# One step of eight transformer batches: the router part of the shared feed-forward computed in two groups of tokens, and GpSimd's scaling of the normalised rows placed behind a rotary sum

## The chip, the cores and the metric

The program runs on one NeuronCore of one Trainium2 chip. The metric is the device time of one execution in microseconds (us). Five engines work beside each other: TensorE (PE in the profile, with its weight loads as PEld), VectorE (DVE), ScalarE (ACT), GpSimd (POOL) and SyncE (SP, which here only starts transfers). They meet through semaphores.

## The reference

An adaptive-normalisation transformer block over 8 batches of 512 tokens by 256 features, all in float32: low-rank attention, then a mixture of 16 experts with a shared feed-forward.

```
h = layernorm(x) * (1 + ca) + sa
x = x + ga * attention(h)              # 16 heads, rotary part of 64, low-rank keys, causal
h = layernorm(x) * (1 + cb) + sb
scores = softmax(h @ gate_w.T)         # 16 experts, the best 4 of each token
y = sum over the 4 experts of weight * (silu(h @ w_gate) * (h @ w_up)) @ w_down
shared = silu(h @ sw_gate) * (h @ sw_up) @ sw_down     # 352 inner features
x = x + gb * (y + shared)
```

sa, ca, ga, sb, cb, gb are six modulation vectors of each batch. An expert takes at most 128 tokens, the first of all 4096 in order that choose it.

## The kernel before, in words

Nothing schedules this program: each engine's instructions are written out in the order in which they run, in one function per engine, and every dependence is a semaphore wait in that text. The 512 tokens of a batch are 4 tiles of 128. The 16 heads are 8 pairs. PSUM is one tensor `PS` of 8 banks of 128 x 512 float32.

For each batch the engines go through eight `step`s, one per head pair (project the next pair's queries, scores, maxima, exponentials, transposes, values), and then a `middle`, which ends the attention of batch b and prepares batch n = b + 1. There are seven such middles in the loop, and an eighth, the last, which has no next batch (`pre` is False). The middle is the place of the change. On TensorE it does, in this order:

- the next batch's low-rank projections (L815), the last pair's values (L695), the output projection by token tile (`output`, L785), and transposes of keys and latents (L834);
- `q_project(0, ..., (0, 1))` (L626 to L630), the first pair's queries of the next batch, first half, into bank 6;
- `turn_h2` (L761): transposes of the second normalised rows `h2`, tiles 0 to 2, into banks 1 and 2. It waits for `n2_ready`, which DVE raises behind `normed` (L1173);
- `q_project(0, ..., (2, 3))`, second half, into bank 7;
- `turn_h2_last` (L766): transposes of tile 3 into bank 0, behind the second `n2_ready`;
- `ffn(b, 2, (3, 4))` (L776, L778): the third part of the shared feed-forward, 96 inner features, whose weights carry the 16 router columns beside them. All 512 tokens are the moving columns, two halves of the 256 features are summed, and each waits for its half of `h2T`;
- `q_turn` (L639): eight transposes of the first pair's queries, which wait for `nope_ready` and `rope_ready`;
- `ffn` parts 0 and 1, with the transposes of the router's logits (L800) between them, and then the first scores of the next batch.

A float32 matmul over features is two instructions in the trace (the two `ffn` lines each issue one pair per half of the features).

ScalarE copies between: `turned_h2` (L1024) writes `h2T` for tiles 0 to 2 with the modulation folded in, `turned_h2_last` (L1030) for tile 3, then `nope_copy` (L951) copies the unrotated half of the queries out of banks 6 and 7 and raises `nope_ready`, and then come `tanh_gate` (L1010) and the router's logits (L1062).

VectorE normalises tile 3 (L1173) and then runs `q_rope`: it waits for `nope_ready`, makes three products out of PSUM (L1196 to L1198) and adds the two halves in SBUF (L1210), which raises `rope_ready`. After that come `silu_mid` (L1282, L1284), `q_low` (L1248) and the router's scores.

GpSimd raises the normalised rows to a power for the standard deviation (L464), and once `h2` has been transposed it multiplies `h2` by the modulation row (L483) and adds the other (L485), 1024 elements a partition each, for SyncE to store as the rows that the experts gather later. Then it copies `x_in` to `x_res` (L489). After the last middle the experts run: GpSimd scatters the tokens' entries, gathers rows, and TensorE computes expert by expert.

`x1_ready` counts the three pieces of the residual of a batch that DVE has formed out of PSUM; the third piece reads bank 3.

Of the kernel before, what the change touches and what calls it, by code (L numbers as in the profile page):

```python
# [23 lines left out]
P = 128  # L24
# [53 lines left out]
def adaln_block(nc, x, wkva, wqnT, wqpe, wkT, wvT, wo, qgam, kgam, sgate, sup, sdown,  # L78
# [21 lines left out]
    with ExitStack() as ctx:  # L100
# [330 lines left out]
        def _(pool):  # L431
# [42 lines left out]
            def post(b, n):  # L474

                wait_alone(pool, var2_ready, NT * b + 3)
                root(rstd2[:, 0:3], mv2[:, 0:3, 1], LN_EPS, eps2, rs2_ready, 2 * b)
                wait_alone(pool, var2_ready, NT * (b + 1))
                root(rstd2[:, 3:], mv2[:, 3:, 1], LN_EPS, eps2, rs2_ready, 2 * b + 1)
                spread = lambda i: modb[:, i, :].unsqueeze(1).to_broadcast([P, NT, H])  # L480
                pool.wait_ge(n2_ready, 2 * (b + 1))
                pool.wait_ge(h2T_ps, 3 * (b + 1))
                pool.tensor_tensor(h2[:], h2[:], spread(2), ALU.mult).then_inc(h2_scaled, 1)  # L483
                pool.wait_ge(h2_scaled, b + 1)
                pool.tensor_tensor(h2[:], h2[:], spread(1), ALU.add).then_inc(h2_ready, 1)  # L485
                if n is not None:
                    wait_alone(pool, x1_ready, 3 * (b + 1))
                    wait_alone(pool, x_landed, (b + 2) * 16)
                    pool.tensor_copy(x_res[:], x_in[:]).then_inc(res_ready, 1)  # L489
# [90 lines left out]
        def _(pe):  # L580
# [188 lines left out]
            def ffn(b, m, banks):  # L769

                off, w = MT[m]
                wide = w + (NE if m == 2 else 0)
                for c in range(2):
                    if m == 2:
                        pe.wait_ge(h2T_ready, 4 * b + c + 3)
                    pe.matmul(PS[0:wide, banks[0], :], sg_sb[:, c, off:off + wide], h2T[:, c, :],  # L776
                              start=c == 0, stop=c == 1)
                    mm = pe.matmul(PS[0:w, banks[1], :], su_sb[:, c, off:off + w], h2T[:, c, :],  # L778
                                   start=c == 0, stop=c == 1)
                mm.then_inc(gu_ps, 1)  # L780

            def output(t, bank, pairs):

# [19 lines left out]
            def middle(b, n, post, pre):  # L803

                if pre:
                    pe.wait_ge(hT_ready, 2 * (n + 1))
                    if not post:
                        pe.wait_ge(wk_in, 4 * 16)
                        pe.wait_ge(wql_ready, 1)
                    for k, t in enumerate(KV_ORDER):  # L810
                        if post:
                            pe.wait_ge(*((pT_act, 4 * n * NPAIR - 1), (pT_dve, 2 * n * NPAIR - 1),
                                         (pT_act, 4 * n * NPAIR), (pT_dve, 2 * n * NPAIR))[k])
                        for c in range(2):
                            mm = pe.matmul(PS[:, t, 0:FW], hT[:, c, bass.ts(t, P)], wkva_sb[:, c, :],  # L815
                                           start=c == 0, stop=c == 1)
                        mm.then_inc(kv_ps, 1)
                if post:
                    values(b * NPAIR + NPAIR - 1, b)
                    pe.wait_ge(oT_ready, (b + 1) * NPAIR)  # L820
                    output(1, 7, (NPAIR - 2,))
                    output(0, 6, range(0, NPAIR - 1))
                    pe.wait_ge(oT_ready, (b + 1) * NPAIR + 1)
                    output(1, 7, (NPAIR - 1,))
                    output(0, 6, (NPAIR - 1,)).then_inc(attn_ps, 1)
                    output(2, 5, range(0, 2))
                else:
                    absorb_output()
                    pe.wait_ge(wvo_ready, 4)
                if pre:  # L830
                    pe.wait_ge(k_ready, n + 1)
                    for bank, src in ((2, kmat[:]), (1, qn[:, :, 0:P]), (0, qn[:, :, P:2 * P])):
                        for t in range(NT):
                            mm = pe.transpose(PS[:, bank, bass.ts(t, P)], src[:, t, :], ident[:])  # L834
                        mm.then_inc(kq_ps, 1)
                if not post:
                    pe.wait_ge(wql_ready, 4)
                if post:
                    output(2, 5, range(2, NPAIR)).then_inc(attn_ps, 1)
                    output(3, 3, range(NPAIR)).then_inc(attn_ps, 1)  # L840
                if pre:
                    pe.wait_ge(kql_ready, 3 * (n + 1))
                    q_project(0, n * NPAIR, (0, 1))
                if post:
                    pe.wait_ge(n2_ready, 2 * b + 1)
                    turn_h2()
                if pre:
                    q_project(0, n * NPAIR, (2, 3))
                if post:
                    pe.wait_ge(n2_ready, 2 * b + 2)  # L850
                    turn_h2_last()
                    ffn(b, 2, (3, 4))
                if pre:
                    q_turn(n * NPAIR)
                if post:
                    if pre:
                        ffn(b, 0, (5, 0))
                    turn_router(b)
                    if not pre:
                        ffn(b, 0, (5, 0))  # L860
                    pe.wait_ge(mid_ready, 3 * b + 1)
                    ffn(b, 1, (3, 4))
                    pe.wait_ge(mid_ready, 3 * b + 2)
                    pe.wait_ge(ls_ready, b + 1)
                if not pre:
                    ranks(b)
                if pre:
                    scores(n * NPAIR, True, (0, 1, 2))
                else:
                    pe.wait_ge(mid_ready, 3 * b + 3)  # L870
                    shared_down(0)
                    pe.wait_ge(slot_ready, b + 2)
                    shared_down(1)
# [64 lines left out]
        def _(act):  # L938
# [88 lines left out]
            def turned_h2_last(b):  # L1027
                act.wait_ge(h2T_ps, 3 * b + 3)
                for c in range(2):
                    act.activation(h2T[:, c, S - P:S], PS[:, 0, bass.ts(c, P)], ACT.Identity,  # L1030
                                   scale=mod2[:, 2 + c:3 + c], bias=mod2[:, c:c + 1]).then_inc(h2T_ready, 1)

            def middle(b, n, post, pre):
# [19 lines left out]
                    act.activation(ql1t[QR:P, :], PS[QR:P, 0, :], ACT.Copy).then_inc(kqh_ready, 1)  # L1053
                if post:
                    turned_h2(b)
                    turned_h2_last(b)
                if pre:
                    nope_copy(n * NPAIR)
                if post:
                    tanh_gate(b, 0, 2, 3)  # L1060
                    w = MT[2][1]
                    act.activation(lgT[:], PS[w:w + NE, 3, :], ACT.Copy).then_inc(lg_ready, 1)  # L1062
# [471 lines left out]
```

## Time and profile before

| | us |
|---|---|
| median of 3 runs | 1312.83 |
| lowest and highest run | 1309.52, 1313.0 |
| the profiled execution | 1317.52 |
| its span, first to last instruction | 1315.6 |

The profiled execution is 1.92 us longer than its span, and 4.69 us (0.36%) above the median of the other runs. In the span PE is busy for 91%, DVE 64%, ACT 51% and POOL 24%; the mean granted TensorE clock is 0.956 of full speed. In the page's 40 slices PE is nine tenths busy or more from the third to the 35th (66 to 1151 us), and the experts' part at the end is sparse on every engine. Idle time in brackets in a row stands just before its first instruction, with what ended it.

### The profile page before, as it was taken

How to read it: one execution, taken by the hardware profiler on the slowest of the kernel's cores; microseconds unless marked ns; L12 is line 12 of the kernel's file. 1: busy time of each engine (PE TensorE's matmuls, PEld its weight loads, DVE VectorE, ACT ScalarE, POOL GpSimd, SP SyncE). 2: the span in 40 equal slices, each digit the busy share in tenths (PEclk: the TensorE clock that was granted, in tenths of full speed). 3: DMA queues.
4: the chain of work that ended last, by engine and by line, in shares of the span. 5: the costliest groups of instructions: out<-in, count | busy, mean ns of one | idle time of the engine just before them, and what ended most of it. 6: DMA issues, size and time to landing. Idle time of an engine off the chain costs nothing.

```text
span 1315.6 us, 25838 instructions
## 1 busy us (share of the span) xinstructions
PE 1193.0 (91%) x7492; PEld 954.0 (73%) x7492; DVE 840.3 (64%) x2575; ACT 667.9 (51%) x1922; POOL 311.8 (24%) x366
## 2 busy tenths in 40 slices
PE   6699999999999999999999999999999999982672
PEld 4488867887688768886888778876887688741341
DVE  3367757776777668766877577767776687641221
ACT  1367635764466536762576356744666367610210
POOL 1000031221312122113221222213221222125674
PEclk7789999999999999999999999999999999986886
DMA  9100002000010001000100020000100010005563
GB/s 306 40 1 0 0 6 60 0 0 0 16 48 0 0 16 48 0 0 16 48 0 0 0 64 0 0 0 16 48 0 0 16 32 1 0 20 144 146 132 47
DMA packets 44853, 41.86 MB, mean 32 GB/s; under 512 B 10800, under 2 KB 41496, under 8 KB 44832
## 3 DMA queue, kind: packets, MB, share of 16 engines
q1 hardware_dynamic: 24864, 26.58, 6.7%
q0 software_dynamic: 7936, 6.38, 2.9%
q10 hardware_dynamic: 12032, 8.65, 2.3%
q8 instruction: 10, 0.16, 0.1%
q14 instruction: 11, 0.09, 0.0%
HBM read 30.84 MB, written 10.81 MB: 32 GB/s over the span
## 4 chain that ended last, share of the span: by engine, by line
PE 76%; DVE 8%; issue 5%; POOL 4%; DMA 3%; ACT 2%; POOLq 0%; DVEq 0%; SPq 0%; ACTq 0%
PE PS L674 10%; PE PS L695 10%; PE PS L653 7%; PE PS L654 6%; PE PS L655 6%; PE PS L785 6%; PE PS L639 4%; PE PS L815 3%; PE PS L793 3%; PE PS L776 2%; PE PS L626 2%; DMA out<-x_res,toku 2%; PE PS L629 2%; PE PS L627 2%; PE PS L630 2%
## 5 line engine op out<-in xcount | busy, mean ns | idle before, releaser
L961 ACT ACTIVATE probs<-probs,nmax 128x512 f32<-128x512 f32 (+3 forms) x512 | 283.1, 554 | 126.7 <-DVE nmax L1217 123.4
L1217 DVE CUSTOM_DVE_ANT_0 probs<-PS,cmask 128x512 f32<-128x512 f32 (+3 forms) x512 | 229.4, 488 | 101.2 <-PE PS L655 98.3
L527 POOL DMA_INDIRECT tab_dram<-entry,slot x128 | 126.1, 985 | 404.5 <-PE PS L695 372.0
L653 PE MATMUL PS<-kTh,qTh 128*128 128x512 f32 (+3 forms) x512 | 178.8, 349 | 1.2 <-DVE qTl L1248 0.6
L970 ACT ACTIVATE pT<-PS 128x384 f32<-128x384 f32 (+3 forms) x320 | 127.7, 462 | 78.9 <-PE PS L674 78.8
L674 PE MATMUL PS<-ident,probs 128*128 128x128 f32 x1280 | 166.1, 276 | 0.0
L655 PE MATMUL PS<-kTh,qTl 128*128 128x512 f32 (+3 forms) x512 | 165.4, 323 | 0.0
L654 PE MATMUL PS<-kTl,qTh 128*128 128x512 f32 (+3 forms) x512 | 165.4, 323 | 0.0
L695 PE MATMUL PS<-pT,kmat 128*64 128x512 f32 (+3 forms) x1024 | 152.0, 439 | 0.3 <-issue 0.3
L674 PEld LDWEIGHTS PS<-ident,probs 128*128 128x128 f32 x1280 | 142.8, 141 | 10.3 <-issue 7.4
L695 PEld LDWEIGHTS PS<-pT,kmat 128*64 128x64 f32 x1024 | 68.0, 136 | 76.0 <-issue 62.1
L785 PE MATMUL PS<-wvo,oT 128*128 128x256 f32 x512 | 116.4, 381 | 0.0
L1248 DVE TENSOR_TENSOR qTl<-PS,qTh 128x512 fp32r<-128x512 f32 x128 | 87.3, 687 | 36.2 <-ACT qTh L956 35.3
L653 PEld LDWEIGHTS PS<-kTh,qTh 128*128 128x128 f32 x512 | 97.0, 189 | 15.2 <-issue 5.3
L785 PEld LDWEIGHTS PS<-wvo,oT 128*128 128x128 f32 x512 | 95.4, 190 | 13.7 <-issue 1.4
L1234 DVE COPY pT<-PS 128x512 f32<-128x512 f32 (+2 forms) x192 | 81.5, 462 | 33.3 <-PE PS L674 31.3
L655 PEld LDWEIGHTS PS<-kTh,qTl 128*128 128x128 f32 x512 | 97.1, 190 | 5.6
L654 PEld LDWEIGHTS PS<-kTl,qTh 128*128 128x128 f32 x512 | 97.3, 190 | 4.5 <-issue 1.7
L961 ACT ACTIVATION_READ_ACCUMULATOR probs<-probs,nmax 128x1 f32 x512 | 95.8, 187 | 0.0
L639 PE MATMUL PS<-ident,qtok 128*128 128x128 f32 x512 | 67.5, 275 | 14.0 <-DVE qtok L1210 14.0
L462 POOL TENSOR_SCALAR rstd<-mv 128x4 f32<-128x4 f32 (+2 forms) x24 | 5.5, 231 | 309.6 <-DVE mv L1169 187.3
L626 PE MATMUL PS<-wq0h,ql0h 128*128 (+1 forms) x256 | 75.7, 296 | 2.2 <-DVE ql1s L1388 2.2
(216 smaller groups left out, 2155.0 us busy)
## 6 DMA issues: line engine op xcount, KB each, us to landing
x_in<-in_x SPq DMA_DIRECT2D x8, 512.0 KB, 5.8
modb<-mod_dram SPq DMA_DIRECT2D x8, 512.0 KB, 5.4
h_dram<-h SPq DMA_DIRECT2D x8, 512.0 KB, 2.9
out<-base SPq DMA_DIRECT2D x8, 512.0 KB, 3.4
pT<-in_wo SPq DMA_DIRECT2D x1, 2048.0 KB, 11.9
tab_dram<-entry,slot POOLq DMA_INDIRECT x128
oT<-in_wqnT SPq DMA_DIRECT2D x1, 1536.0 KB, 10.1
pT<-in_egate ACTq DMA_DIRECT2D x6, 176.0 KB
```

The lines of the kernel that those rows point to most:

```text
L527: pool.indirect_dma_start(tab_dram[:, :], bass.IndirectOffsetOnAxis(ap=slot[:, j:j + 1], axis=0), entry[:, j, :], None, bounds_check=NE * ...
L626: pe.matmul(dst, ql0h[:, tok], wq0h[:, cols], start=True, stop=False)
L639: mm = pe.transpose(PS[:, QBANKS[h], bass.ts(t, P)], qtok[:, 2 * t + h, :], ident[:])
L653: pe.matmul(PS[:, bank, 0:n], qTh[:, h, rows_q], kTh[:, 0:n], start=True, stop=False)
L654: pe.matmul(PS[:, bank, 0:n], qTh[:, h, rows_q], kTl[:, 0:n], start=False, stop=False)
L655: pe.matmul(PS[:, bank, 0:n], qTl[:, h, rows_q], kTh[:, 0:n], start=False, stop=True).then_inc(s_ps, 1)
L674: mm = pe.transpose(PS[:, bank, col:col + P], probs[:, UO[u] + j * P:UO[u] + (j + 1) * P], ident[:])
L695: mm = pe.matmul(PS[h * KL:(h + 1) * KL, OBANK, j * P:S], kmat[:, j, 0:KL], pT[:, h, j, j * P:S], start=j == 0, stop=j == NT - 1)
L785: mm = pe.matmul(PS[:, bank, 0:H], oT[:, p, bass.ts(t, P)], wvo[:, p, :], start=p == 0, stop=p == NPAIR - 1)
L961: act.activation(probs[:, UO[u]:UO[u] + UW[u]], probs[:, UO[u]:UO[u] + UW[u]], ACT.Exp, scale=-1.0, bias=nmax[:, u:u + 1], accum_out=psums ...
L970: cp = act.activation(pT[:, h, 0:i + 1, bass.ts(i, P)], PS[:, bank, col:col + UW[u]].rearrange("p (j q) -> p j q", q=P), ACT.Copy)
L1217: dve.tensor_tensor_reduce(out=probs[:, UO[u]:UO[u] + UW[u]], in0=PS[:, SBANK[u], 0:UW[u]], in1=cmask[:, S - UW[u]:S], scale=-1.0, scalar= ...
```

## The change

```diff
--- before.py
+++ after.py
@@ -480,6 +480,8 @@
                 spread = lambda i: modb[:, i, :].unsqueeze(1).to_broadcast([P, NT, H])
                 pool.wait_ge(n2_ready, 2 * (b + 1))
                 pool.wait_ge(h2T_ps, 3 * (b + 1))
+                if n is not None:
+                    wait_alone(pool, rope_ready, n * NPAIR + 1)
                 pool.tensor_tensor(h2[:], h2[:], spread(2), ALU.mult).then_inc(h2_scaled, 1)
                 pool.wait_ge(h2_scaled, b + 1)
                 pool.tensor_tensor(h2[:], h2[:], spread(1), ALU.add).then_inc(h2_ready, 1)
@@ -769,15 +771,24 @@
             def ffn(b, m, banks):
 
                 off, w = MT[m]
-                wide = w + (NE if m == 2 else 0)
                 for c in range(2):
-                    if m == 2:
-                        pe.wait_ge(h2T_ready, 4 * b + c + 3)
-                    pe.matmul(PS[0:wide, banks[0], :], sg_sb[:, c, off:off + wide], h2T[:, c, :],
+                    pe.matmul(PS[0:w, banks[0], :], sg_sb[:, c, off:off + w], h2T[:, c, :],
                               start=c == 0, stop=c == 1)
                     mm = pe.matmul(PS[0:w, banks[1], :], su_sb[:, c, off:off + w], h2T[:, c, :],
                                    start=c == 0, stop=c == 1)
                 mm.then_inc(gu_ps, 1)
+
+            def ffn_router(b, part, banks):
+
+                off, w = MT[2]
+                lo, hi = (0, S - P) if part == 0 else (S - P, S)
+                for c in range(2):
+                    pe.wait_ge(h2T_ready, 4 * b + 2 * part + c + 1)
+                    pe.matmul(PS[0:w + NE, banks[0], lo:hi], sg_sb[:, c, off:off + w + NE], h2T[:, c, lo:hi],
+                              start=c == 0, stop=c == 1)
+                    mm = pe.matmul(PS[0:w, banks[1], lo:hi], su_sb[:, c, off:off + w], h2T[:, c, lo:hi],
+                                   start=c == 0, stop=c == 1)
+                return mm
 
             def output(t, bank, pairs):
 
@@ -847,9 +858,11 @@
                 if pre:
                     q_project(0, n * NPAIR, (2, 3))
                 if post:
+                    pe.wait_ge(x1_ready, 3 * b + 3)
+                    ffn_router(b, 0, (3, 4))
                     pe.wait_ge(n2_ready, 2 * b + 2)
                     turn_h2_last()
-                    ffn(b, 2, (3, 4))
+                    ffn_router(b, 1, (3, 4)).then_inc(gu_ps, 1)
                 if pre:
                     q_turn(n * NPAIR)
                 if post:
@@ -1053,10 +1066,10 @@
                     act.activation(ql1t[QR:P, :], PS[QR:P, 0, :], ACT.Copy).then_inc(kqh_ready, 1)
                 if post:
                     turned_h2(b)
-                    turned_h2_last(b)
                 if pre:
                     nope_copy(n * NPAIR)
                 if post:
+                    turned_h2_last(b)
                     tanh_gate(b, 0, 2, 3)
                     w = MT[2][1]
                     act.activation(lgT[:], PS[w:w + NE, 3, :], ACT.Copy).then_inc(lg_ready, 1)
```

`ffn` keeps parts 0 and 1. Part 2, with the router's columns, becomes `ffn_router`, which takes a group of tokens: group 0 is tokens 0 to 383, group 1 tokens 384 to 511. Group 0 is put ahead of the wait for the last normalised tile. In the loop's seven middles all parts of the change act; the last middle has no next query, so there only the split is different.

On TensorE, the stretch between the second half of the next query's projection (last row L630 before, L632 now) and the transposes of the query. Before:

```order
L630 MATMUL PS<-wq1l,ql1s 128x256
L850 REGISTER_ALU
L766 MATMUL PS<-ident,h 128x128 [waits n2_ready]
L766 MATMUL PS<-ident,h 128x128
L775 ISA
L776 MATMUL PS<-h2T,sg_sb 112x512 [waits h2T_ready]
L778 MATMUL PS<-h2T,su_sb 96x512
L775 REGISTER_ALU
L776 MATMUL PS<-h2T,sg_sb 112x512 [waits h2T_ready]
L778 MATMUL PS<-h2T,su_sb 96x512
L639 MATMUL PS<-ident,qtok 128x128 [waits rope_ready,nope_ready]
```

Now, up to the first product of group 1:

```order
L861 ISA
L786 ISA [waits x1_ready]
L787 MATMUL PS<-h2T,sg_sb 112x384 [waits h2T_ready]
L789 MATMUL PS<-h2T,su_sb 96x384
L786 REGISTER_ALU
L787 MATMUL PS<-h2T,sg_sb 112x384 [waits h2T_ready]
L789 MATMUL PS<-h2T,su_sb 96x384
L863 REGISTER_ALU
L768 MATMUL PS<-ident,h 128x128 [waits n2_ready]
L768 MATMUL PS<-ident,h 128x128
L786 REGISTER_ALU
L787 MATMUL PS<-h2T,sg_sb 112x128 [waits h2T_ready]
```

Group 0's four products of 384 columns have moved ahead of the wait for `n2_ready`, behind a new wait for `x1_ready`; behind the transposes of tile 3 four products of 128 columns are left, and the query's transposes follow them with their waits unchanged.

On ScalarE, from the first half of `h2T` (tiles 0 to 2) to the router's logits. Before:

```order
L1024 ACTIVATE h2T<-PS,mod 128x384 [waits h2T_ps]
L1023 REGISTER_ALU
L1024 ACTIVATE h2T<-PS,mod 128x384 [waits h2T_ps]
L1028 REGISTER_ALU
L1030 ACTIVATE h2T<-PS,mod 128x128 [waits h2T_ps]
L1030 ACTIVATE h2T<-PS,mod 128x128
L950 ISA
L951 ACTIVATE qtok<-PS 128x8x64 [waits q_ps]
L1010 ACTIVATE th<-PS 96x512 [waits gu_ps]
L1062 ACTIVATE lgT<-PS 16x512
```

Now:

```order
L1037 ACTIVATE h2T<-PS,mod 128x384 [waits h2T_ps]
L1036 REGISTER_ALU
L1037 ACTIVATE h2T<-PS,mod 128x384 [waits h2T_ps]
L963 ISA
L964 ACTIVATE qtok<-PS 128x8x64 [waits q_ps]
L1041 REGISTER_ALU
L1043 ACTIVATE h2T<-PS,mod 128x128 [waits h2T_ps]
L1043 ACTIVATE h2T<-PS,mod 128x128
L1023 ACTIVATE th<-PS 96x512 [waits gu_ps]
L1075 ACTIVATE lgT<-PS 16x512
```

The copy of the query's unrotated half (`qtok`) has moved ahead of the two copies of tile 3 and of their wait for `h2T_ps`.

On GpSimd, the scaling of `h2` and what follows. Before:

```order
L482 REGISTER_ALU [waits n2_ready]
L483 TENSOR_TENSOR h<-h,modb 128x1024 [waits h2T_ps]
L485 TENSOR_TENSOR h<-h,modb 128x1024 [waits h2_scaled]
L92 ISA [waits x1_ready,const_ready]
L489 COPY x_res<-x_in 128x1024 [waits x_landed,const_ready]
```

Now:

```order
L482 REGISTER_ALU [waits n2_ready]
L92 ISA [waits h2T_ps]
L485 TENSOR_TENSOR h<-h,modb 128x1024 [waits rope_ready,const_ready]
L487 TENSOR_TENSOR h<-h,modb 128x1024 [waits h2_scaled]
L92 ISA [waits x1_ready,const_ready]
L491 COPY x_res<-x_in 128x1024 [waits x_landed,const_ready]
```

The multiplication waits for `rope_ready` as well, and the addition and the copy of `x_in` stay queued behind it.

## Rows read from the trace of the kernel before

**Rows 1.** The page's table of busy time, PE, DVE, ACT, POOL.

```profile
PE 1193.0 (91%) x7492; PEld 954.0 (73%) x7492; DVE 840.3 (64%) x2575; ACT 667.9 (51%) x1922; POOL 311.8 (24%) x366
```

**Rows 2.** Chain that ended last, 155 to 235 us: start us, us, what.

```profile
191.25 0.45 ACT h2T L1030
...
193.60 2.67 DVE qtok L1210
...
197.47 0.86 PE PS L776 x2
```

**Rows 3.** Timeline of PE, 180 to 216 us: start us, us, engine line op.

```profile
189.27 0.28 PE L630 MATMUL PS<-wq1l,ql1s 128*128 128x256 f32 x1
190.41 0.44 PE L766 MATMUL PS<-ident,h 128*128 128x128 f32 x2 [0.86 <-DVE h L1173]
191.40 1.11 PE L776 MATMUL PS<-h2T,sg_sb 128*112 128x512 f32 x2 [0.55 <-ACT h2T L1030]
...
196.40 1.06 PE L639 MATMUL PS<-ident,qtok 128*128 128x128 f32 x8 [1.32 <-DVE qtok L1210]
```

**Rows 4.** Timeline of ACT, 186 to 212 us.

```profile
188.07 1.23 ACT L1024 ACTIVATE h2T<-PS,mod 128x384 f32<-128x384 f32 x2 [6.27 <-PE PS L761]
190.89 0.81 ACT L1030 ACTIVATE h2T<-PS,mod 128x128 f32<-128x128 f32 x2 [1.58 <-PE PS L766]
191.59 0.59 ACT L951 ACTIVATE qtok<-PS 128x512 f32<-128x512 f32 x1
```

**Rows 5.** Timeline of DVE, 189 to 216 us.

```profile
189.94 0.41 DVE L1173 TENSOR_SCALAR h<-x,mv,rstd 128x256 f32<-128x256 f32 x1 [1.08 <-POOL rstd L464]
192.21 0.69 DVE L1196 TENSOR_TENSOR qr<-PS,cos_sb 128x512 f32<-128x512 f32 x1 [1.86 <-ACT qtok L951]
...
193.60 2.66 DVE L1210 TENSOR_TENSOR qtok<-qr 128x512 f32<-128x512 f32 x1
196.18 0.67 DVE L1282 SCALAR_TENSOR_TENSOR mid<-th,PS 96x512 f32<-96x512 f32 x1
```

**Rows 6.** Timeline of POOL, 184 to 240 us.

```profile
190.93 2.36 POOL L483 TENSOR_TENSOR h<-h,modb 128x1024 f32<-128x1024 f32 x1 [1.02 <-PE PS L766]
193.37 2.34 POOL L485 TENSOR_TENSOR h<-h,modb 128x1024 f32<-128x1024 f32 x1
195.66 1.50 POOL L489 COPY x_res<-x_in 128x1024 f32<-128x1024 f32 x1
```

**Rows 7.** L1210: ns min/median/max of one; then its group: busy us, mean.

```profile
L1210 DVE TENSOR_TENSOR qtok<-qr x64: 691/693/2661, 61.6 to 1132.8; 128x512 f32<-128x512 f32 x64
...
L1210 DVE TENSOR_TENSOR qtok<-qr 128x512 f32<-128x512 f32 x64 | 58.1, 907 | 2.2
```

**Rows 8.** Stretches: length, busy PE, PEld, DVE, ACT, POOL, granted clock, DMA.

```profile
189.50:196.40 6.90, 4.17 (x11) 1.50 (x11) 4.56 (x6) 2.48 (x5) 5.80 (x4) 1.00 0.00 0
...
1032.40:1039.30 6.90, 4.21 (x11) 1.48 (x10) 4.53 (x6) 2.48 (x5) 5.80 (x4) 1.00 0.00 0
```

**Rows 9.** Timeline of PE, 158 to 216 us: a stream of 256 columns.

```profile
173.71 5.45 PE L785 MATMUL PS<-wvo,oT 128*128 128x256 f32 x24
```

**Rows 10.** Timeline of PE, 1160 to 1178 us, the last middle.

```profile
1163.28 0.87 PE L761 MATMUL PS<-ident,h 128*128 128x128 f32 x6 [0.79 <-DVE h L1173]
1166.18 0.69 PE L766 MATMUL PS<-ident,h 128*128 128x128 f32 x2 [2.02 <-DVE h L1173]
1167.41 2.05 PE L776 MATMUL PS<-h2T,sg_sb 128*112 128x512 f32 x2 [0.55 <-ACT h2T L1030]
```

**Rows 11.** Timeline of all engines, 1148 to 1194 us, the last middle.

```profile
1163.92 1.23 ACT L1024 ACTIVATE h2T<-PS,mod 128x384 f32<-128x384 f32 x2 [14.92 <-PE PS L761]
...
1173.48 0.59 ACT L1010 ACTIVATE th<-PS 96x512 f32<-96x512 f32 x1 [5.77 <-PE PS L778]
```

**Rows 12.** Busy time in stretches of the last middle, then granted clock.

```profile
1164.20:1166.20 2.00, 0.02 (x1) 0.03 (x1) 0.87 (x3) 0.96 (x2) 0.80 (x2) 0.79 0.00 0
...
1168.00:1170.00 2.00, 2.00 (x3) 0.57 (x2) 0.00 (x0) 0.00 (x0) 1.92 (x2) 0.50 0.00 0
```

## The prediction

> **What bounds the kernel now.** I read the page's table first: PE is busy for 91% of the span [rows 1], so what shortens the program must take work or idle time from PE. The chain that ended last then shows where PE lets go of it: in the middle between two batches it leaves PE for a copy on ScalarE, later for the rotary sum on VectorE, and only then comes back to PE for good (the reader should see the 2.67 us of L1210 in it) [rows 2]. PE's timeline gives the sizes. The last matmul of the query's projection starts at 189.27; then come 0.86 us idle for the normalised tile 3, two transposes, 0.55 us idle for ScalarE's copy, the router part (`ffn` part 2), and 1.32 us idle until the rotary sum is there; `q_turn` starts at 196.40 [rows 3]. So the piece that I cost runs from 189.4 (one pace of 0.12 us behind the last start) to 196.40: 7.0 us, of which 2.73 us are idle.
>
> Why is the sum late? Its copy on ScalarE stands behind both copies of tile 3 and starts at 191.59, though its queries lay in PSUM by 189.55 (189.27 and 0.28) [rows 3, 4]. And the sum itself lasts 2.66 us where the median of its line is 0.69 [rows 5, 7]. The group's total of 58.1 us is 64 times 0.693 (44.4) and 13.7 more, seven times 1.97: once in each of the seven loop middles [rows 7].
>
> **What the sum meets on GpSimd.** It starts at 193.60, when L485 runs there (193.37 to 195.71), and ends at 196.26, 0.55 us behind it. The product out of PSUM that runs beside L483 (L1196) has its usual 0.69, and so has `silu_mid` beside the copy L489 (0.67) [rows 5, 6]. The operation with both inputs in SBUF is stretched, those with one in PSUM are not.
>
> **The change, part by part, in a loop middle.**
>
> Group 0 first. It needs the copies of tiles 0 to 2, 188.07 to 189.30 [rows 4], and `x1_ready`, whose work on DVE lies ahead of the normalising that starts at 189.94 and of its power on GpSimd; both are there at 189.4. A pair of instructions with 512 columns takes 0.86 us on the chain [rows 2]; with 384 columns three quarters, 0.64, and four pairs 2.57. PE is through at 189.40 + 2.57 = 191.97. The tile was normalised at 190.35 [rows 5], so this wait is gone, but the transposes come 1.56 us later than now, at 191.97.
>
> From the start of these transposes to the first `ffn` product PE took 0.99 us (190.41 to 191.40) [rows 3], and nothing covers it now either: first product of group 1 at 192.96.
>
> Group 1 is eight instructions of 128 columns. The rows show none of that shape. The nearest are the transposes of `q_turn`, also 128 columns: eight take 1.06 us with the last one's tail in it [rows 3]. The stream of 256 columns takes 0.22 each (5.45 us for 24, less its tail) [rows 9]; half of that by columns is 0.11, eight of them 0.90 us, and that is the lower end. The upper end is as long as 256 columns, 1.8 us. I take 0.90, since the transposes are the nearest and lie at it. The second half of tile 3's copy is ready 0.4 us behind the first [rows 4], inside the first four of these, and adds no wait. `q_turn` could start at 193.86.
>
> Does the sum hold it up? The copy of the unrotated half now starts when the projection is complete, 189.6, and lasts 0.59: 190.2. DVE is in the normalising until 190.35, and from the start of L1196 to that of the sum it took 1.39 us (192.21 to 193.60) [rows 5]: the sum runs from 191.8 to 192.5 with its undisturbed 0.69. That is 1.4 us ahead of `q_turn`, which then waits for PE alone. Tile 3's copies find ScalarE free.
>
> GpSimd: it would be released by the transposes at 192.4 anyway, and the added wait lets it go at 192.5. Behind it are queued L485 and L489, so it ends near 198.5 where it ended at 197.16 [rows 6], 3.9 us later against PE's new clock of events. The next thing asked of it is the count of the router's choices, which follows the scores of the next batch's first pair; I cost this at nothing. If its cover were gone, SyncE's store of `h2` would be late by 1.6 us, with a whole batch until the rows are written again.
>
> Sum for a loop middle: 196.40 - 193.86 = 2.54; I take off 0.04 for the added semaphore instructions and write 2.5. In seven middles 17.5 us; with group 1 at the upper end 7 x 1.6 = 11.2. Behind `q_turn` PE runs the other parts of the shared feed-forward without a gap, and the copies and `silu_mid` that it needs follow PE's own events, so I expect the 2.5 us to be kept.
>
> **The last middle.** There PE idles 2.02 us for tile 3 and the granted clock then falls: 0.79 in the two microseconds of idling, 0.50 in the stretch behind, which is the lower level, 1.2 GHz. The router part starts at 1167.41 and its result is read at 1173.48 [rows 10 to 12]. Now group 0 can start when the first half of the copies is there, 1163.92 + 0.6 = 1164.55, and fill the idle time. At full clock: 1164.6 + 2.57 + 0.99 + 0.90 + 0.3 to the reader = 1169.4, a gain of 4.1 us. If the clock falls all the same when group 0 starts, all of it doubles but ScalarE's part: 1164.6 + 5.14 + 1.23 + 1.80 + 0.3 = 1173.1, a gain of 0.4. The gaps that are left (0.8, 0.4 and 0.6 us) are like those in the loop middles (0.86, 0.55, 1.32), where the clock stays 1.00 [rows 3, 8]; so I take 4.1. The Trainium skill, "TensorE: Matmul & The Clock Gate", section "Why this matters for your kernels", warns of long PE-idle gaps between bursts only; by it nothing would fall with gaps this short (4.1), while this trace shows a fall already behind 2.02 us, which keeps 0.4 as the other end. Routing, scattering and the experts follow this result one after the other, so the gain should pass through.
>
> Sum: 17.5 + 4.1 = 21.6 us. Against the profiled execution, 1317.5 - 21.6 = 1295.9; its time stands 0.36% above the median of the runs, so for the median I write 1312.8 - 21.6 = 1291.2.
>
> **One rule against the change's own reason.** By the rows, the sum starts at 191.8, ahead of any release of GpSimd, and one that has started could still be stretched, to 194.5 if by the same 1.97 us; that is 0.6 us behind 193.86, and it is what the new wait on GpSimd is worth at most: 4 us in seven middles. The Trainium skill ("SBUF — State Buffer", "Who interferes with whom") says that a VectorE instruction with two SBUF inputs and a GpSimd one that reads SBUF exclude each other, and that the one issued second waits for the whole first. By it the wait is worth nothing once the sum comes first, and the gain is wholly that of the order on PE and ScalarE. The trace agrees as far as it goes: an end 0.55 us behind L485's. The time forecast is the same by both.
>
> **The rivals.**
>
> A, group 1 is dear: small products at 0.22 us each, or waits between them. For it: no row of this shape. Against: the transposes of 128 columns. Time: 1312.8 - 7 x 1.6 - 3.2 = 1298.4. Chance 0.13.
>
> B, the clock falls in the last middle: 1312.8 - 17.5 - 0.4 = 1294.9. Chance 0.24.
>
> C, the gain is given back: GpSimd's work, now beside `silu_mid` and `q_low`, stretches these as it did the sum, or an engine that was level with PE in the next batch's first step takes over. If all 17.5 go, 1308.7. Against: `silu_mid` ran beside L489 in 0.67. Chance 0.05.
>
> D, slower. The place is the loop middle, behind group 0; the mechanism is the clock. PE's order of work and idling changes, and if the clock falls as it does in the last middle, it does so with dense work behind it. The price is one microsecond for each microsecond of full-clock work done at the lower level. It decides from 2.5 us of such work in a middle, and with the 9.0 us from group 1 to the next scores it is 6.5 us a middle: 1312.8 + 45.5 = 1358. Against: the clock was 1.00 with 2.73 us of idling in all seven, and now it is about 0.6. Chance 0.03.
>
> **How the numbers follow.** The forecast has the remaining 0.55. The range goes from 1287, where middles give 2.8 (the handover of 0.99 or the small products slightly quicker) and the runs' own spread of 3.5 us helps, to 1301, where A and B come together (1312.8 - 11.2 - 0.4 = 1301.2). About 0.3% (3.9 us) is what a measurement here can tell from no change: beyond 1308.9 is only D, and near it C. Faster 0.94, same 0.03, slower 0.03.
>
> **What would show it.** In a loop middle: the sum 0.69 us in all 64, no idle time before `q_turn` and none before the last transposes, `q_turn` 4.5 us behind the projection's last matmul, GpSimd's L483 released just behind the sum, clock 1.00. In the last middle: the clock, and `th` 4 us earlier. It would be wrong if `q_turn` still waited for DVE, if 128-column products took over 0.2 us each, or if the next batch's first scores did not come 2.5 us earlier.

## The result and the profile after

The changed kernel runs at 1293.27 us, median of 5 runs (1290.29 to 1294.04), against 1312.83 us of the kernel before (5 runs beside them, 1309.52 to 1313.27): a ratio of 0.9851 with a 95% interval of 0.9833 to 0.9868, 19.6 us less. The profiled execution took 1294.04 us, its span is 1292.1. The prediction was 1291.2 within 1287 to 1301.

The page's busy times, which answer to [rows 1]: PE is busy 9 us less, with the same columns streamed: 2.7 us less in the seven loop middles and 2.6 in the last, where the clock was down before, but also 3.0 in steps of the loop that the change does not touch and 0.9 behind the last middle. The section after this one takes the spans apart in the same way.

```profile
PE 1183.8 (92%) x7556; PEld 958.6 (74%) x7556; DVE 824.9 (64%) x2575; ACT 667.9 (52%) x1922; POOL 309.3 (24%) x366
```

PE's timeline in the first middle, which answers to [rows 3]; this execution entered it 0.45 us later than the one before. Lines of the file have moved by 2 to 13: L632 is the end of the query's projection, L787 and L789 are `ffn_router`, L768 the transposes of tile 3, L641 `q_turn`, L775 `ffn`.

```profile
189.72 0.28 PE L632 MATMUL PS<-wq1l,ql1s 128*128 128x256 f32 x1
189.84 0.81 PE L787 MATMUL PS<-h2T,sg_sb 128*112 128x384 f32 x2
...
191.78 0.81 PE L789 MATMUL PS<-h2T,su_sb 128*96 128x384 f32 x2
192.42 0.38 PE L768 MATMUL PS<-ident,h 128*128 128x128 f32 x2
193.35 0.47 PE L787 MATMUL PS<-h2T,sg_sb 128*112 128x128 f32 x2 [0.55 <-ACT h2T L1043]
...
194.10 0.38 PE L789 MATMUL PS<-h2T,su_sb 128*96 128x128 f32 x2
194.32 1.04 PE L641 MATMUL PS<-ident,qtok 128*128 128x128 f32 x8
195.19 1.02 PE L775 MATMUL PS<-h2T,sg_sb 128*128 128x512 f32 x2
```

From the last start of the projection to `q_turn` it is 4.60 us (189.72 to 194.32) where it was 7.13 (189.27 to 196.40). The idle times of 0.86 and 1.32 us are gone and the 0.55 us in front of group 1 are left. Group 1's eight instructions take 0.97 us (193.35 to 194.32), their steady pace 0.11 each (193.66, 193.88, 194.10).

ScalarE, DVE and GpSimd in the same stretch, which answer to [rows 4], [rows 5] and [rows 6]:

```profile
190.04 0.60 ACT L964 ACTIVATE qtok<-PS 128x512 f32<-128x512 f32 x1 [0.29 <-PE PS L632]
...
190.71 0.68 DVE L1209 TENSOR_TENSOR qr<-PS,cos_sb 128x512 f32<-128x512 f32 x1
...
192.09 0.69 DVE L1223 TENSOR_TENSOR qtok<-qr 128x512 f32<-128x512 f32 x1
...
192.84 0.81 ACT L1043 ACTIVATE h2T<-PS,mod 128x128 f32<-128x128 f32 x2 [2.20 <-PE PS L768]
193.08 2.38 POOL L485 TENSOR_TENSOR h<-h,modb 128x1024 f32<-128x1024 f32 x1 [2.73 <-PE PS L768]
...
195.14 0.68 DVE L1295 SCALAR_TENSOR_TENSOR mid<-th,PS 96x512 f32<-96x512 f32 x1 [2.36 <-ACT th L1023]
...
195.54 2.36 POOL L487 TENSOR_TENSOR h<-h,modb 128x1024 f32<-128x1024 f32 x1
...
195.86 0.68 DVE L1297 TENSOR_TENSOR midT<-mid,PS 96x512 f32<-96x512 f32 x1
...
196.46 1.28 DVE L1261 TENSOR_TENSOR qTl<-PS,qTh 128x512 fp32r<-128x512 f32 x2
...
197.83 1.04 POOL L491 COPY x_res<-x_in 128x1024 f32<-128x1024 f32 x1
```

The sum (L1223) runs from 192.09 to 192.78 in its usual 0.69 us, 1.5 us ahead of `q_turn`; GpSimd's two operations follow at 193.08. `silu_mid` (L1295, L1297) and `q_low` (L1261) now run beside them in their usual times, and the copy (L491) lasts 1.04 us where it lasted 1.50 [rows 6]. The line of the sum over the whole program, which answers to [rows 7]:

```profile
L1223 DVE TENSOR_TENSOR qtok<-qr x64: 691/691/693, 62.1 to 1111.5; 128x512 f32<-128x512 f32 x64
```

Two lines from the list of PE's waits (us in total, times, longest). `q_turn` (L641) waits for the sum twice, at 62.91 and 76.40 us in the first batch and in no middle, where the kernel before waited nine times and 14.0 us; the wait for tile 3's normalising is on no line of the list:

```profile
PE PS L641 <- DVE qtok L1223: 4.8, 2, 2.9
PE PS L787 <- ACT h2T L1043: 4.4, 8, 0.6
```

PE in the last middle, which answers to [rows 10]:

```profile
1141.99 0.87 PE L763 MATMUL PS<-ident,h 128*128 128x128 f32 x6 [0.79 <-DVE h L1186]
1143.45 0.87 PE L787 MATMUL PS<-h2T,sg_sb 128*112 128x384 f32 x2 [0.59 <-ACT h2T L1037]
...
1146.09 0.38 PE L768 MATMUL PS<-ident,h 128*128 128x128 f32 x2
1147.02 0.47 PE L787 MATMUL PS<-h2T,sg_sb 128*112 128x128 f32 x2 [0.55 <-ACT h2T L1043]
...
1149.45 0.42 PE L811 MATMUL PS<-ident,lgT 16*128 16x16 f32 x4 [1.30 <-ACT lgT L1075]
```

and its granted clock, behind the other columns of the stretches, 1.00 where it was 0.50 to 0.79 [rows 12]:

```profile
1142.00:1146.00 4.00, 3.41 (x14) 2.04 (x15) 1.71 (x5) 1.23 (x2) 0.81 (x2) 1.00 0.00 0
1146.00:1150.00 4.00, 2.15 (x16) 1.58 (x15) 0.10 (x1) 1.99 (x4) 3.30 (x2) 1.00 0.00 0
```

### The profile page after: what moved, and what is told of

The parts are those of the page before. It is cut to its first block, busy times and chain, and to the rows that moved or that the text cites. A ratio compares the mean times of both kernels' runs of the same rounds, so it can differ in the third digit from the quotient of the medians.

```text
span 1292.1 us, 26002 instructions
## 1 busy us (share of the span) xinstructions
PE 1183.8 (92%) x7556; PEld 958.6 (74%) x7556; DVE 824.9 (64%) x2575; ACT 667.9 (52%) x1922; POOL 309.3 (24%) x366
## 4 chain that ended last, share of the span: by engine, by line
PE 82%; issue 4%; DMA 4%; DVE 4%; POOL 3%; ACT 2%; POOLq 0%; DVEq 0%; SPq 0%; ACTq 0%
PE PS L676 11%; PE PS L697 10%; PE PS L796 8%; PE PS L655 7%; PE PS L656 6%; PE PS L657 6%; PE PS L641 4%; PE PS L826 3%; PE PS L804 3%; DMA out<-x_res,toku 3%; PE PS L628 2%; PE PS L631 2%; PE PS L632 2%; PE PS L629 2%; PE PS L630 2%
## 5 line engine op out<-in xcount | busy, mean ns | idle before, releaser
L1261 DVE TENSOR_TENSOR qTl<-PS,qTh 128x512 fp32r<-128x512 f32 x128 | 87.1, 685 | 35.4 <-ACT qTh L969 35.4
L655 PEld LDWEIGHTS PS<-kTh,qTh 128*128 128x128 f32 x512 | 97.1, 190 | 12.5 <-issue 4.4
L1256 DVE TENSOR_TENSOR oT<-PS,th 128x512 f32 (+1 forms) x64 | 43.7, 683 | 51.0 <-PE PS L697 51.0
## 6 DMA issues: line engine op xcount, KB each, us to landing
oT<-in_wqnT SPq DMA_DIRECT2D x1, 1536.0 KB, 10.5
```

Of the source, the lines that this page charges most:

```text
L655: pe.matmul(PS[:, bank, 0:n], qTh[:, h, rows_q], kTh[:, 0:n], start=True, stop=False)
L1261: dve.tensor_tensor(qTl[:, h, :], PS[:, QBANKS[h], :], qTh[:, h, :].bitcast(F32), ALU.subtract).then_inc(qTl_ready, 1)
```

## Where the 23.5 us between the two profiles are

The spans differ by 23.5 us, the medians by 19.6, so I took single executions apart before crediting the change. For each trace I read from PE's timeline the starts of `turn_h2` in the eight middles and of each pair's `values` (the 16 instructions of L695 in the kernel before), and from ScalarE's and DVE's those of the first `th` and of the cast in the last middle. Five quantities come of it: a loop middle with the step that follows (from `turn_h2` to the next `values`), the sum over the seven batches between the first and the last `turn_h2`, in the last middle the router part (from `turn_h2` to `th`) and all up to the tokens' slots (the start of DVE's cast to `slot`, L1336), and everything behind that. The other rows belong to the experiments below.

| profile | loop middle | first to last turn_h2 | last middle: turn_h2 to th | turn_h2 to slots | slots to the end |
|---|---|---|---|---|---|
| before | 38.60 to 38.66 | 975.74 | 10.20 | 21.23 | 131.1 |
| before, second (e8_before) | 38.60 to 38.67 | 977.08 | 9.13 | 20.15 | 131.2 |
| the change | 36.03 to 36.11 | 954.00 | 6.19 | 17.23 | 132.9 |
| the change, second (e0_after) | 36.03 to 36.10 | 957.15 | 6.20 | 18.30 | 132.6 |
| the change, third (e9_after) | 36.03 to 36.09 | 958.58 | 6.20 | 18.23 | 133.6 |
| e1_no_wait | 36.02 to 36.10 | 957.82 | 6.20 | 17.23 | 131.6 |
| e2_wait_only | 37.09 to 37.15 | 958.81 | 9.30 | 20.32 | 133.7 |
| e3_copy_only | 37.09 to 37.16 | 958.76 | 7.60 | 18.62 | 130.8 |
| e4_split_only | 41.81 to 43.12 | 1002.30 | 6.20 | 18.29 | 130.3 |
| e5_split_wait | 38.15 to 39.62 | 972.34 | 6.19 | 18.29 | 133.7 |
| e6_last_only | 38.59 to 38.65 | 969.37 | 6.20 | 17.21 | 129.4 |
| e7_turn_first | 35.56 to 35.63 | 948.07 | 6.20 | 17.23 | 132.9 |
| e10_turn_first | 35.55 to 35.61 | 953.84 | 6.20 | 17.22 | 133.3 |

The loop middle repeats to some hundredths of a microsecond in every execution and on every chip, except in e4 and e5, where the clock falls in it, and it moved by 2.57 us: 18.0 us in seven. The rest of the batch differs where the code is the same. The five steps between the middles, which no kernel here touches, take 12.20 us each on the chip that ran e2, e3, e6 and e7, and anything from 12.19 to 12.51, a few times 13.1, in the other traces: the kernel before has 975.74 on one chip, and the same loop code in e6 969.37 on another. Everything behind the slots scatters between 129.4 and 133.7. So of the 23.5 us the loop's middles are 18.0, the last middle 4.0, and 1.5 scatter (3.7 in the steps, -1.8 behind the slots, and -0.4 in front of the first middle).

## The experiments

Theory 1: the gain is that of the order on TensorE and ScalarE, 2.5 us in a loop middle, and GpSimd's wait adds nothing once the sum runs first. Its rivals: the wait (the free sum) carries the gain; the split carries it by itself; an instruction that has started is stretched all the same.

**e0_after: the change again**, on the chip of e1, e4 and e5.

> The changed kernel again, to be compared with the others on the same chip, and a second profile of it. Theory 1 (the gain is that of the order on TensorE and ScalarE: 2.5 us in each of seven middles and 4 us in the last): about 0.985 of before. The first profile showed the batches behind the middle 3.7 us shorter in sum than in the profile of before, in steps that the change does not touch; if that belongs to the change it is here again, if it is scatter of single executions it is not.

Measured: ratio 0.9843 (0.9824 to 0.9862). Loop middle as in the first profile; the steps behind it scattered more than there. They were shorter by accident in the profile of after, and the 3.7 us are not the change's: without the middles, first to last `turn_h2` is 705.3 us before, 701.6 in the first profile of the change and 704.7 here.

**e1_no_wait: without GpSimd's wait.**

```diff
-                if n is not None:
-                    wait_alone(pool, rope_ready, n * NPAIR + 1)
```

> The change without GpSimd's wait for the rotary sum. Theory 1 (the sum starts 0.6 us before GpSimd is released, and whichever instruction comes second waits for the other): sum at 0.69 us in all 64, time as with the wait, within 0.1%. Rival (a sum that has started is stretched all the same, or GpSimd gets in first): sum up to 2.66 us in the seven middles, q_turn up to 0.6 us later in each, 4 us in all.

Measured: ratio 0.9833 (0.9812 to 0.9853), the loop middle 36.02 to 36.10, and the sum never over 0.693 us:

```profile
L1221 DVE TENSOR_TENSOR qtok<-qr x64: 691/692/693, 59.6 to 1112.7; 128x512 f32<-128x512 f32 x64
```

Lines of DVE, PE and GpSimd in the first middle show why. The sum ends at 190.13, and the transposes release GpSimd at 190.22:

```profile
189.44 0.69 DVE L1221 TENSOR_TENSOR qtok<-qr 128x512 f32<-128x512 f32 x1
189.76 0.38 PE L766 MATMUL PS<-ident,h 128*128 128x128 f32 x2
...
190.22 2.35 POOL L483 TENSOR_TENSOR h<-h,modb 128x1024 f32<-128x1024 f32 x1 [2.53 <-PE PS L766]
```

The sum starts 0.78 us before GpSimd's operation and is done 0.09 us before it, in all seven middles. With the wait GpSimd starts 0.66 us behind the start of the transposes (189.56 and 190.22 in e0_after), without it 0.46: the wait holds GpSimd back by 0.2 us and gains nothing. It guards an order that PE's own work already gives, by 0.1 us. Since the two never overlap here, e1 does not show what would happen to a sum that GpSimd joins; e3 does.

**e2_wait_only: the kernel before with that wait alone.**

```diff
                 pool.wait_ge(h2T_ps, 3 * (b + 1))
+                if n is not None:
+                    wait_alone(pool, rope_ready, n * NPAIR + 1)
```

> The kernel before with GpSimd's wait alone. The sum then lasts 0.69 us and is ready at 194.3, the undivided router part ends at 194.95: q_turn there instead of at 196.40, 1.4 us in each of seven middles, 10 us in all: 1303. Rival (another wait takes its place): less than 4 us.

Measured: ratio 0.9940 (0.9927 to 0.9954), 7.9 us. The loop middle is 37.12 instead of 38.64: 1.52 us, 10.6 in seven. `q_turn` follows the router part with no idle time in front of it:

```profile
193.94 1.04 PE L641 MATMUL PS<-ident,qtok 128*128 128x128 f32 x8
```

The runs gave 2.7 us less than 10.6, which lies outside their interval (6.0 to 9.6) and is more than I can place, since e3 below has the same middle on the same chip and gave all of it; this profile's part behind the slots is 2.6 us longer than that of before, and the table's spread there is as large. In the kernel before, the wait alone carries three fifths of what the whole change carries in a middle.

**e3_copy_only: the kernel before with ScalarE's copy moved ahead of tile 3's copies.**

```diff
                 if post:
                     turned_h2(b)
-                    turned_h2_last(b)
                 if pre:
                     nope_copy(n * NPAIR)
                 if post:
+                    turned_h2_last(b)
                     tanh_gate(b, 0, 2, 3)
```

> The kernel before with ScalarE's copy of the query moved ahead of the copies of tile 3, nothing else. The sum starts at 191.8 while GpSimd's first operation (190.9 to 193.3) runs. Theory 1 (the second waits for the first to end, then runs): sum of about 2.0 us, ready at 193.9, behind it the router part until 194.95, so q_turn again 1.4 us earlier: 1303, with a stretched sum that costs nothing. Rival (stretched by both of GpSimd's operations): sum until 196.3, q_turn as before, 1313.

Measured: ratio 0.9920 (0.9906 to 0.9933), 10.5 us, and the loop middle 37.12, the very gain of e2, with the sum stretched. DVE, GpSimd and PE in the first middle:

```profile
190.95 2.35 POOL L483 TENSOR_TENSOR h<-h,modb 128x1024 f32<-128x1024 f32 x1 [1.02 <-PE PS L766]
...
191.67 2.17 DVE L1210 TENSOR_TENSOR qtok<-qr 128x512 f32<-128x512 f32 x1
...
193.38 2.68 POOL L485 TENSOR_TENSOR h<-h,modb 128x1024 f32<-128x1024 f32 x1
...
194.94 1.04 PE L639 MATMUL PS<-ident,qtok 128*128 128x128 f32 x8
```

The sum comes at 191.67 during L483, which ends at 193.30, and ends at 193.84, 0.54 us behind it. Now L485 is the one that waits: it starts at 193.38, with the sum under way, and lasts 2.68 us where 2.34 is its time, while the sum is not stretched by it. So whichever comes first keeps the other out for that one instruction, as the Trainium skill has it ("SBUF — State Buffer", "Who interferes with whom"). The trace agrees, in both directions. The kernel before shows the second direction too: its copy L489 starts at 195.66, before the sum ends at 196.26, and lasts 1.50 us [rows 5, 6], 1.03 to 1.05 in every trace where no sum runs beside it. And the two cures should not add up: either frees `q_turn` of the sum, and then it follows the router part without idle time, which only the split shortens. Both together without the split were not run.

**e4_split_only: only the split**, with ScalarE's order as before and no wait on GpSimd (the diff against the change is that of e1 together with e3's, reversed).

> Only the router part's split; ScalarE's copy of the query stays behind the copies of tile 3, and GpSimd does not wait. Theory 1: the copies of tile 3 come 1.9 us later, the sum would start near 195.2 on the first middle's clock, meets GpSimd's second operation and ends 0.5 us behind it near 197.8; q_turn 1.3 us later than before in each of seven middles (9 us lost), last middle 4 us gained: 1318, slower than before by 5. Rival (the split carries the gain by itself): 1293 to 1300.

Measured: ratio 1.0149 (1.0125 to 1.0174), 19.6 us slower than before, four times what was expected. The loop middle is 41.81 to 43.12, 3.2 to 4.5 us more than before and not 1.3. The timeline of PE, DVE and GpSimd in the first middle has both parts of it:

```profile
191.72 0.38 PE L787 MATMUL PS<-h2T,su_sb 128*96 128x128 f32 x2
...
192.95 2.34 POOL L485 TENSOR_TENSOR h<-h,modb 128x1024 f32<-128x1024 f32 x1
193.18 2.65 DVE L1221 TENSOR_TENSOR qtok<-qr 128x512 f32<-128x512 f32 x1
...
195.98 1.92 PE L639 MATMUL PS<-ident,qtok 128*128 128x128 f32 x8 [3.88 <-DVE qtok L1221]
...
197.70 1.89 PE L773 MATMUL PS<-h2T,sg_sb 128*128 128x512 f32 x2
...
199.41 1.04 PE L775 MATMUL PS<-h2T,su_sb 128*128 128x512 f32 x2
```

From `turn_h2` (185.62) to `q_turn` it is 10.36 us, against 8.86 before: 1.5 us, as the theory had it. But PE now idles 3.88 us in one piece, and what follows runs at half speed: `q_turn` takes 1.92 us where it takes 1.06, the next product 1.89 where it takes 1.02. The stretches (length, busy PE, PEld, DVE, ACT, POOL, granted clock, DMA):

```profile
192.00:195.90 3.90, 0.11 (x1) 0.00 (x0) 3.87 (x5) 1.18 (x2) 3.82 (x3) 1.00 0.00 0
195.90:199.30 3.40, 3.32 (x10) 2.42 (x11) 2.60 (x4) 1.19 (x2) 0.83 (x1) 0.52 0.46 154
199.30:203.00 3.70, 3.70 (x13) 1.61 (x12) 0.42 (x3) 0.60 (x1) 0.00 (x0) 0.98 0.00 0
```

The clock is at its lower level, 1.2 GHz, for 3.4 us behind the gap, and that costs 1.7; over the seven middles, 1.7 to 3.0. It is the mechanism of the rival that ends slower, set off by a longer wait in a kernel that has only part of the change.

**e5_split_wait: split and GpSimd's wait, ScalarE's order as before** (the diff is e3's, reversed, against the change).

> The split and GpSimd's wait, with the copy of the query behind the copies of tile 3 as before. Theory 1: sum of 0.69 us from 195.2 to 195.9, q_turn at 196.0, 0.4 us earlier than before in each middle, last middle 4 us gained: 1306. Rival (the wait carries the gain, 1.97 us in each middle): 1295.

Measured: ratio 0.9983 (0.9966 to 0.9999), 2.2 us. The sum is never over 0.693, and six of the seven loop middles are 38.15 to 38.18, 0.46 below before, as expected. The first is 39.62:

```profile
193.85 1.94 PE L641 MATMUL PS<-ident,qtok 128*128 128x128 f32 x8 [1.92 <-DVE qtok L1223]
```

There the idle time of 1.92 us was enough for the clock to fall (eight transposes in 1.94 us). 0.46 in six middles less 1.0 in one is 1.8, and by the table the last middle, at 18.29 us up to the slots against 18.62 to 21.23 without the split, adds 0.3 to 2.9. So even with GpSimd's wait the split is worth almost nothing in the loop unless the copy comes first.

**e6_last_only: the split where `pre` is False alone**, the loop as before. Of its diff against the change this is TensorE's part; `whole_router` is part 2 undivided, as before, and GpSimd's wait and ScalarE's new order are taken back too. Lines that only moved to the right are shown as unchanged.

```diff
+                    if not pre:
                         pe.wait_ge(x1_ready, 3 * b + 3)
                         ffn_router(b, 0, (3, 4))
                     pe.wait_ge(n2_ready, 2 * b + 2)
                     turn_h2_last()
-                    ffn_router(b, 1, (3, 4)).then_inc(gu_ps, 1)
+                    if pre:
+                        whole_router(b, (3, 4))
+                    else:
+                        ffn_router(b, 1, (3, 4)).then_inc(gu_ps, 1)
```

> The split in the last middle alone; loop middles as before. If the last middle is worth what the profile of the changed kernel shows: router result 4 us earlier, clock 1.00 throughout, 1308.8. Rival (the clock's fall depends on where the kernel stands, and full clock there was luck): 0.4 to 2.4 us.

Measured: ratio 0.9973 (0.9964 to 0.9982), 3.5 us (2.4 to 4.7), between the 4 that was expected and the rival's 0.4 to 2.4. All nine traces with the split have 6.19 or 6.20 us from `turn_h2` to `th`. The four without it have 10.20, 9.13, 9.30 and 7.60, all with the same idle time of 2.02 us. e3's is the one in which the clock did not fall; its PE lines answer to [rows 10]:

```profile
1149.21 0.44 PE L766 MATMUL PS<-ident,h 128*128 128x128 f32 x2 [2.02 <-DVE h L1173]
1150.20 1.11 PE L776 MATMUL PS<-h2T,sg_sb 128*112 128x512 f32 x2 [0.55 <-ACT h2T L1030]
...
1152.86 1.02 PE L778 MATMUL PS<-h2T,su_sb 128*96 128x512 f32 x2
```

The first pair takes 1.11 us where it took 2.05 [rows 10]. So the split by itself is worth 1.4 us there (7.60 - 6.20), and 1.5 to 2.6 more in the executions in which the clock falls. Against that, the clock fell one gap later in four of the nine split traces, behind the 1.30 us in which PE waits for the router's logits, and behind the same 1.30 us in none of the four without it. In e0_after, the change again, the transposes of the logits (L811) and the product behind them show it, and the stretch:

```profile
1149.74 0.42 PE L811 MATMUL PS<-ident,lgT 16*128 16x16 f32 x4 [1.30 <-ACT lgT L1075]
1150.09 1.94 PE L775 MATMUL PS<-h2T,sg_sb 128*128 128x512 f32 x2
```

```profile
1149.80:1153.20 3.40, 3.40 (x8) 1.64 (x9) 2.80 (x13) 0.26 (x1) 1.88 (x1) 0.57 0.16 55
```

These four take 18.2 to 18.3 us from `turn_h2` to the slots and the other five 17.2: 1.05 us given back. The means over all traces are 20.08 without and 17.69 with the split, 2.4 us, from four and nine executions; the runs of e6 gave 3.5, and 2.4 is the lower end of their interval.

**e8_before and e9_after: both kernels again**, beside the last experiment.

> The kernel before, for a second profile beside the two below on one chip. If the scatter of the steps between the middles and the clock in the last middle belong to the execution and not to the code: loop middles as in the first profile (38.6 us from turn_h2 to the next values), the steps behind them at any values from 12.2 to 12.5, the last middle's router result 7.6 to 10.2 us behind its turn_h2 by the clock. Ratio 1.000 within 0.2%.

> The changed kernel on the chip of the next one: ratio 0.984 to 0.986, router result 6.2 us behind turn_h2 in the last middle, 36.06 us from turn_h2 to the next values in the others.

Measured: 0.9993 (0.9980 to 1.0005) and 0.9835 (0.9817 to 0.9854). Their traces stand in the table, and both answer to what was expected.

**e7_turn_first and e10_turn_first: `q_turn` in the gap that is left.** The sum is ready when tile 3's transposes end, so the query's transposes can fill the time in which PE waits for ScalarE's copy.

```diff
                     turn_h2_last()
-                    ffn_router(b, 1, (3, 4)).then_inc(gu_ps, 1)
                 if pre:
                     q_turn(n * NPAIR)
+                if post:
+                    ffn_router(b, 1, (3, 4)).then_inc(gu_ps, 1)
```

> The change, and the transposes of the query put ahead of the router part of the last 128 tokens. The sum is ready at 192.8 when the transposes of tile 3 end, so the eight transposes fill the 0.55 us in which TensorE waits for ScalarE's copy: 0.5 us in each of seven middles, 3.5 to 3.9 us in all: 1289.5. Rival (the router's result, 0.3 us later, or a late qTh becomes the wait): no gain.

> The change with the query's transposes ahead of the last 128 tokens' router part, on the same chip as the change: 3.3 us faster than it (0.47 in each of seven middles), ratio 0.002 to 0.003 below the change's. Rival (the profile's gain is given back in the runs): equal.

Measured: e7 0.9833 (0.9819 to 0.9846) on its chip, where the change itself was not run, so that its ratio alone shows no gain over the change's 0.9835 to 0.9851 elsewhere; beside the change, e10 1291.72 us against 1295.10, ratios 0.9817 (0.9795 to 0.9839) and 0.9835. The loop middle is 35.56 to 35.63 in both traces, 0.48 below the change: 3.4 us, the same as the medians, though the intervals overlap. PE's lines show no idle time left between the projection and the first scores:

```profile
189.75 0.38 PE L768 MATMUL PS<-ident,h 128*128 128x128 f32 x2
190.26 1.06 PE L641 MATMUL PS<-ident,qtok 128*128 128x128 f32 x8
191.16 0.38 PE L787 MATMUL PS<-h2T,sg_sb 128*112 128x128 f32 x2
...
192.03 1.02 PE L775 MATMUL PS<-h2T,sg_sb 128*128 128x512 f32 x2
```

By the medians beside each other it is the fastest version tried.

## Why the prediction was right

**The loop middle** was right term by term. Four pairs of 384 columns: 2.57 us forecast, 2.58 measured (189.84 to 192.42). From the transposes to group 1: 0.99 forecast, 0.93. Group 1: 0.90 forecast from the transposes' pace, 0.97. The sum's end ahead of `q_turn`: 1.4 us forecast, 1.5. 2.54 was the sum for a middle and 2.53 is what the first one shows; I had taken off 0.04 for added semaphore instructions, which are not to be seen. In seven middles 18.0 us against 17.5, read in three traces of the change.

**What the change leaves to GpSimd** was right: `silu_mid` and `q_low` keep their times beside its operations, and the queue behind the new wait ended at 198.87 and held nobody up: the whole gain is still there at the next `values`, 36 us behind `turn_h2`. Rival C has nothing for it.

**The rule against the wait** came out right, in two parts. e1 shows that the wait is worth nothing: without it the sum, the middle and the time are the same. But there the sum is over 0.09 us before GpSimd starts, so e1 alone would also fit a sum that can be stretched once it has started; that it cannot is shown by e3, where L485 joins the sum under way and the sum still ends 0.54 us behind L483. In e2 the same wait is worth 1.52 us in a middle. A wait's worth depends on what else moves.

**The last middle** is the term whose reasoning did not hold. 4.1 us were taken, as if the kernel before always lost the clock there, and that this profile pair shows 4.0 is luck of two executions. The gain of the order is 1.4 us, and the rest is what a fallen clock costs the kernel before in that one execution. I read a row at the lower clock as a property of the kernel; three further traces with the same idle time show 0, 1.5 and 1.7 us of it where this one has 2.6. What the term is worth on the average stays between two measures: the means up to the slots give 2.4 us, the runs of e6 give 3.5 (2.4 to 4.7), which does not exclude 4.1. With 18.0 from the middles the total is 20.4 to 21.5; three comparisons of the change with before gave 19.6 (17.3 to 21.9), 20.7 and 21.7.

**Rival A** fell with the pace of 0.11. **Rival B**, the clock falling in the last middle when group 0 starts, happened in none of nine traces; in four it fell behind group 1 and cost 1.05 us, which neither forecast nor rival had. **Rival D**'s mechanism exists, and I had looked for it in the wrong place: the new order leaves 0.55 us of idle time in a loop middle, and the clock was 1.00 in all 21 loop middles of the change's three traces. It comes up in e4 and once in e5, where the split pushes ScalarE's copy and so the sum further back and makes one long idle time out of several short ones. With 1.5 us of wait and 1.7 to 3.0 of clock it turns a part of this change, taken alone, into 19.6 us lost.

**What stays open.** Why the untouched steps take 12.20 us on one chip and up to 12.5 on others, and why what follows the slots scatters by 4 us, was not tried; nor was why the runs of e2 show 2.7 us less than its loop middles, or what decides in which execution the clock falls behind the same idle time. The 18.0 us of the loop middles do not hang on it; the worth of the last middle does.

## What to carry to other kernels

Cost each part of a change of order alone as well as together: here the split alone loses 19.6 us, the wait alone gains 8 and the copy alone 10.5, the pair of split and copy 22, and all three together 20 to 22, the same within the intervals. Where work is pushed ahead of another engine's release, look at which in-order queue the released work shares with something critical, since what the first gains can be lost in that queue. Compare stretches between two fixed instructions over several traces before crediting a difference of spans to a change.

## What the runs showed of the hardware

The granted clock falls behind an idle time of PE, but not by its length alone. 3.88 us: it fell in seven of seven middles (e4; each is 3.2 us or more above before, of which the wait explains 1.5), in four of them within the idle time and in three right behind its end. 2.02 us, in the last middle without the split: in three of four. 1.92 us: in one of seven (e5). 1.32 us, with 0.86 and 0.55 close in front: in none of the 21 loop middles of before, e8_before and e6_last_only. And 1.30 us behind the shorter bursts of the split last middle: in four of nine; behind the undivided router part: in none of four. While it is down, work takes twice as long: the first of e4's middles does in 3.4 us what takes 1.7, and over its seven middles the idle time of 3.9 us costs another 1.7 to 3.0. I had not expected the fall behind 2 us to be a matter of the single execution.

VectorE's sum with both inputs in SBUF and GpSimd's operation exclude each other in both directions, one instruction at a time: the sum ended 0.54 us behind the first of GpSimd's operations in e3, and the second, then in its turn the later one, was 0.34 us longer. The one that comes later loses what is left of the first, less 0.1 us: 1.97 us for a sum that finds 2.11 us of L485 left and 0.46 us for a copy that finds 0.60 us of the sum left (both in the kernel before), 0.34 us for an L485 that finds 0.46 us of the sum left (e3).
